# Cross attention steps: maxima of the third tile in front of what a step makes, row scaling and context split in other steps

## The reference, cut to what matters

```python
x = _layernorm(x + attn(x, wq, wk, wv, wo))         # 16 heads of 32, rotary, causal
x = _layernorm(x + xattn(x, ctx, Wq, Wkv, Wout))    # causal: only the first 512 rows of ctx count
x = _layernorm(x + ffn(x, w1, w2, w3))              # w1..w3 = nf4_roundtrip(weight1..3)

# xattn
qp = q @ Wq.T
k, v = split(latent_kv @ Wkv_expand.T, 2)
scores = where(causal, einsum('bhqd,bhkd->bhqk', qh, kh) / sqrt(32), -inf)
out = einsum('bhqk,bhkd->bhqd', softmax(scores), vh) @ Wout.T
```

## Time and profile before

| | us |
|---|---|
| median of 3 runs | 1152.41 (1149.77 to 1152.74) |
| the profiled execution | 1148.54 |
| its span, first to last instruction | 1146.8 |
| batches 4 to 7 (cross attention) | 493.8 to 883 of the span |
| TensorE busy | 1034.3 |
| VectorE busy | 753.6 |
| ScalarE busy | 470.7 |
| GpSimd busy | 457.8 |
| mean granted TensorE clock | 0.975 of full speed |

### The profile page before, as it was taken

One profiled execution on the slowest core, in us unless ns is written; L12 is line 12 of the kernel. 1 busy time (PEld: TensorE's weight loads), 2 busy tenths in 40 slices (PEclk: granted clock), 3 DMA queues, 4 the chain that ended last, 5 costly groups with the idle time before them and its releaser, 6 DMA issues.

```text
span 1146.8 us, 17458 instructions
## 1 busy us (share of the span) xinstructions
PE 1034.3 (90%) x6248; PEld 664.9 (58%) x6248; DVE 753.6 (66%) x1566; ACT 470.7 (41%) x578; POOL 457.8 (40%) x492
## 2 busy tenths in 40 slices
PE   6789898988998898998989889888989999999995
PEld 5545445543555354455556555555646888888884
DVE  6785757656765769548866786887684646364545
ACT  3334353645364556455654555555443211112110
POOL 4446975986289545323242333232367300000000
PEclk9799999999999999999999999999999999999998
DMA  5731466477444854646575565647536301101020
GB/s 207 217 93 31 120 167 171 146 190 211 135 147 121 228 167 125 160 82 162 146 177 126 135 176 141 154 107 196 124 83 204 115 1 57 55 11 64 1 74 37
DMA packets 84290, 145.14 MB, mean 127 GB/s; under 512 B 15416, under 2 KB 32160, under 8 KB 83948
## 3 DMA queue, kind: packets, MB, share of 16 engines
q1 hardware_dynamic: 73180, 111.90, 36.6%
q0 software_dynamic: 9712, 31.34, 9.5%
q10 hardware_dynamic: 1312, 0.79, 0.2%
HBM read 78.09 MB, written 23.73 MB: 89 GB/s over the span
## 4 chain that ended last, share of the span: by engine, by line
PE 47%; DVE 13%; POOL 3%; issue 2%; ACT 2%; DMA 2%; SPq 1%; ACTq 0%; DVEq 0%; POOLq 0%
PE att_pv L1014 7%; PE att_scores L1238 7%; PE att_pv L1238 7%; PE att_scores_T L1268 7%; PE att_scores_T L941 4%; PE att_scores L957 4%; PE att_scores_T L943 3%; PE att_scores_T L942 3%; DVE att_scores L1581 2%; PE att_scores_T L1118 2%; PE att_scores_T L990 2%; DVE att_nf_zone L1737 2%; DVE att_mx L1586 1%; DVE att_x_lo L1526 1%; DMA att_probs<-nf_x 1%
## 5 line engine op out<-in xcount | busy, mean ns | idle before, releaser
L1403 ACT ACTIVATE att_probs<-att_scores_T 128x1024 f32<-128x1024 f32 (+2 forms) x256 | 218.2, 884 | 187.0 <-PE att_scores_T L990 184.2
L1014 PE MATMUL att_pv<-att_probs,att_v 128*32 128x512 f32 (+3 forms) x1024 | 220.0, 546 | 3.8 <-POOL att_probs L796 3.2
L1014 PE MATMUL att_pv<-att_probs,att_ones 128*32 128x512 f32 (+3 forms) x1024 | 219.9, 546 | 0.0
L1586 DVE TENSOR_REDUCE att_mx<-att_scores 128x2 f32<-128x1024 f32 x124 | 151.5, 1222 | 101.1 <-PE att_scores L957 100.4
L957 PE MATMUL att_scores<-att_k_stack,att_q_stack 96*128 96x256 f32 (+1 forms) x504 | 165.5, 401 | 48.3 <-DVE att_mx L1586 21.9
L990 PE MATMUL att_scores_T<-att_q_stack,att_k_stack 97*128 97x512 f32 (+2 forms) x512 | 138.9, 381 | 9.7 <-ACT att_raw L1340 2.3
L1581 DVE CUSTOM_DVE_ANT_0 att_scores<-att_scores,att_cmask 128x128 f32<-128x128 f32 (+3 forms) x256 | 120.4, 508 | 37.0 <-PE att_scores L957 37.0
L957 PEld LDWEIGHTS att_scores<-att_k_stack,att_q_stack 96*128 96x128 f32 x504 | 86.8, 191 | 98.1 <-DVE att_mx L1581 35.3
L796 POOL TENSOR_SCALAR_AFFINE_SELECT att_probs<-att_probs 128x256 f32<-128x256 f32 x128 | 59.2, 463 | 189.2 <-ACT att_probs L1403 186.0
L990 PEld LDWEIGHTS att_scores_T<-att_q_stack,att_k_stack 97*128 97x128 f32 x512 | 85.3, 190 | 52.5 <-issue 17.5
L1487 ACT ACTIVATE att_probs<-att_scores 128x512 f32<-128x512 f32 x44 | 26.3, 598 | 207.7 <-PE att_scores L1238 207.7
(11 more groups left out here) (254 smaller groups left out, 2099.1 us busy)
## 6 DMA issues: line engine op xcount, KB each, us to landing
att_q_stack<-att_q_hi SPq DMA_DIRECT2D x128, 128.0 KB, 3.2
att_probs<-nf_x SPq DMA_DIRECT2D x28, 352.0 KB, 3.6
att_nf_home<-nf_reciprocals POOLq DMA_DIRECT2D x48, 176.0 KB, 4.8
att_q_stack<-att_q_lo SPq DMA_DIRECT2D x64, 128.0 KB, 3.5
att_k_stack<-att_k_hi SPq DMA_DIRECT2D x64, 128.0 KB, 3.4
att_nf_home<-nf_x SPq DMA_DIRECT2D x20, 352.0 KB, 3.7
w_nf<-att_nf_zone SPq DMA_DIRECT2D x192, 22.0 KB, 2.8
att_k_stack<-att_k_hi SPq DMA_DIRECT2D x64, 64.0 KB, 3.3
```

The lines of the kernel that those rows point to most:

```text
L1014: last = T.matmul(pv[HD * j:HD * j + HD, sums, q0:S], lhs, pr[:, at:at + S - q0], start=(t == 0), stop=(t == TT - 1))
L1403: A.activation(probs_of(b, r)[:, 1024 * h:1024 * h + w], bank[:, 0:w], ACT.Exp, scale=SCALE).then_inc(st_free, 1)
L1586: V.tensor_reduce(mx[:, p % 2, :].rearrange("p (r t) -> p r t", r=2)[:, :, t], sco[:, :, :], AX.X, ALU.max).then_inc(sc_free, 1)
```

## The change

Six moves, and no operation is added or taken out:

1. TensorE, step 1 of batches 1 to 7: the third tile's maxima (t = 2) stand ahead of `project_out(b - 1, 0)` and not behind it; VectorE takes them ahead of the round's passes and of the residual.
2. TensorE, cross steps that make something (2 to 6): t = 2 stands ahead of the first half of what is made, and t = 3 between the halves; before it was t = 2 between them and t = 3 behind them. VectorE takes t = 0, 1, 2 in a row, ahead of spread, sums and passes, and t = 3 ahead of the last pass.
3. `scale_rows` of batches 5 and 6 goes from step 5 to step 6, behind `over_sums`, and with it the store on SyncE from step 5 to step 6 (`stored_at`); residual loads go to step 7 (two) and to step 0 (two).
4. `split_context(b + 1)` of batches 4 to 6 goes from the end of step 3 to the end of step 0; GpSimd's `load_context` goes from step 4 to step 1 of the next batch.
5. `begin_spread` in step 3 of cross batches stands behind the maxima of t = 1, and in made steps of t = 2.
6. ScalarE, all cross steps with one round at their end: its pass `exceed(end, 0)` stands behind the fourth exponential, not ahead of it.

```diff
--- before.py
+++ after.py
@@ -148,7 +148,7 @@
 
 def stored_at(b):
 
-    return 5 if late(b) and b != B else 4 if b == B else 3
+    return 6 if B < b < NB - 1 else 5 if late(b) and b != B else 4 if b == B else 3
 
 
 def values_of(b):
@@ -593,9 +593,9 @@
                         scaler_rows(1)
                     if b > 0 and p == stored_at(b):
                         store(b - 1)
-                    for t in {6: (0,), 7: (1, 2)}.get(p, ()) if b != B else ():
+                    for t in (({7: (0, 1)} if B < b < NB - 1 else {6: (0,), 7: (1, 2)}).get(p, ())) if b != B else ():
                         load_residual(b, t)
-                    for t in (3,) if b != B + 1 else range(TT):
+                    for t in range(TT) if b == B + 1 else (2, 3) if b > B + 1 else (3,):
                         if p == 0 and b > 0:
                             load_residual(b - 1, t)
                     if (b, p) == after(*ROUND_STEPS[-1], 1):
@@ -867,7 +867,7 @@
                         pool.wait_ge(st_full, AT["raw", b + 1, f"x{p - 1}"] + 1)
                         if nxt[0] <= NB:
                             load_x(*nxt)
-                    if crossed(b + 1) and b + 2 < NB and p == 4:
+                    if b + 1 == B and p == 4 or crossed(b) and b + 2 < NB and p == 1:
                         pool.wait_ge(c_split, b + 1 - B + 1)
                         load_context(b + 2)
                     if (b, p) == (B - 1, 5):
@@ -1179,20 +1179,27 @@
                     if ahead:
                         weigh(b, p, 0)
                     if p == 1 and b > 0:
+                        maxima(*fore, 2)
                         project_out(b - 1, 0)
-                        maxima(*fore, 2)
                         if mid is not None:
                             rounding(mid)
                         project_out(b - 1, 1)
                         for half in range(2):
                             make(b + 1, whats, half)
+                        maxima(*fore, 3)
+                    elif crossed(b) and whats:
+
+                        maxima(*fore, 2)
+                        make(b + 1, whats, 0)
+                        maxima(*fore, 3)
+                        make(b + 1, whats, 1)
                     else:
                         make(b + 1, whats, 0)
                         if fore and not (crossed(b) and p == 0):
                             maxima(*fore, 2)
                         make(b + 1, whats, 1)
-                    if fore and (whats or p == 1):
-                        maxima(*fore, 3)
+                        if fore and (whats or p == 1):
+                            maxima(*fore, 3)
                     if not ahead:
                         weigh(b, p, 0)
                     weigh(b, p, 1)
@@ -1448,9 +1455,11 @@
                     if mid is not None:
                         for k in scalar_passes(mid):
                             exceed(mid, k)
-                    elif 0 in mine:
+                    elif 0 in mine and not crossed(b):
                         exceed(end, 0)
                     exponential(b, p, 3)
+                    if mid is None and 0 in mine and crossed(b):
+                        exceed(end, 0)
                     if (b, p) == (B - 1, 1):
                         act.wait_ge(wq_in, 32)
                         for h, src in enumerate((rsw, rsum)):
@@ -1801,22 +1810,28 @@
                         turn_first(p - 1)
                     if b > 0 and not late(b) and p == 2:
                         end_spread(range(TT))
-                    if late(b) and p == 3:
+                    if b == B - 1 and p == 3:
                         begin_spread(range(TT))
-                    if (b, p) == (B - 1, 4) or b > B and p == 5:
+                    if (b, p) == (B - 1, 4) or (b, p) == (NB - 1, 5):
                         scale_rows(range(0, 2), TT - 1)
                     if fore:
                         maxima(*fore, 1)
                         largest_behind(b, p, 1)
                     if b > 0 and not late(b) and p == 2:
                         scale_rows(range(TT), TT - 1)
+
+                    quick = crossed(b) and bool(made(b + 1, p))
+                    if quick:
+                        maxima(*fore, 2)
+                    if crossed(b) and p == 3:
+                        begin_spread(range(TT))
                     if late(b) and p == 3:
                         end_spread(range(TT))
                     if b == B and p == 3:
                         scale_rows(range(TT), TT - 1)
                     if b == B - 1 and p == 4:
                         scale_rows(range(2, TT), TT - 1)
-                    if b > B and p == 5:
+                    if (b, p) == (NB - 1, 5):
                         scale_rows(range(2, TT), TT - 1)
                     if p % 2 == 0 and pairs(b, p) > 0:
                         sums_of(G)
@@ -1832,19 +1847,23 @@
                     beside = 0 < b < B - 1 and p == 6
                     if not beside:
                         exceeds(end, (1, 2))
-                    if fore:
+                    if fore and not quick:
                         maxima(*fore, 2)
                         largest_behind(b, p, 2)
+                    if quick:
+                        maxima(*fore, 3)
                     exceeds(end, (1, 2, 3) if beside else (3,))
                     if p % 2 == 0 and pairs(b, p) > 0:
                         over_sums(G)
+                    if B < b < NB - 1 and p == 6:
+                        scale_rows(range(TT), TT - 1)
                     if (b, p) == (0, 2):
                         reciprocals()
                     if crossed(b + 1):
                         for what in made(b + 1, p)[:-1]:
                             cut_raw(b + 1, what)
                     early = bool(made(b + 1, p)) or p == 1
-                    if fore and early:
+                    if fore and early and not quick:
                         maxima(*fore, 3)
                         largest_behind(b, p, 3)
                     if end is not None:
@@ -1857,7 +1876,11 @@
                             cut_raw(b + 1, what)
                         elif what[0] != "v" and b > 0:
                             swap(("raw", b + 1, what))
-                    if crossed(b + 1) and b + 1 < NB and p == 3:
+                    if (b, p) == (B - 1, 3):
+                        split_context(B)
+                    if crossed(b) and b + 1 < NB and p == 0:
+
+                        wait_freed(dve, ("raw", b, "v1"))
                         split_context(b + 1)
             sums_of(KT * NB - 1)
             over_sums(KT * NB - 1)
```

## The result

The changed kernel takes 1167.01 us as a median of four runs (1164.90 to 1169.22), the kernel before 1151.09 us beside it (1147.90 to 1152.74). The ratio is 1.0142 with a 95% interval of 1.0109 to 1.0175, slower by 15.9 us. The forecast was 1168 in a range of 1155 to 1174.

A forecast was written before the change was run, and what follows sets the result against it. TensorE, busy 90% of the span, was taken to bound the kernel, with VectorE setting the pace in steps 2, 4 and 5. Terms summed to +16.3 us on a median of 1152.4, about 1168 us, range 1155 to 1174.

The forecast's parts named there:

- Steps 6 and 7: Batches 5 and 6: rows scaled in step 6 delay the store and SyncE's list behind it; +9.2 and +8.5 us.
- The last term: Batches 5 and 6: from the first pass of step 7 to its end, 4.4 us, ending at 30.0.
- case without the blocking: Rival: rows and GpSimd do not block each other; +8 to +11 us, 1161 to 1163 us; chance 0.22.
- The split: Context split at the end of step 0 meets `weighed`, delaying t = 1 in step 1 of batches 4 to 6; +4.55 us.
- Steps 4: Context split leaves step 4, which gets 1.0 us shorter in each of three batches; -3.0 us.
- ScalarE's pass: Pass behind the fourth exponential: +0.7 us in step 0 of batches 5, 6, 7, +0.3 in step 7 of batch 4; +2.4.
- The clock: Rival: TensorE idles 5 us or more in step 7 and the clock drops behind both long waits; +3, 1171 us; chance 0.10.
- Steps 2, 3, 5 and steps 1 of batches 2 and 3: New maxima order, and rows gone from steps 5: +0.3 steps 2, -0.5 steps 3, -4.7 steps 5, +0.9 those steps 1.
- Step (4, 6): Step 6 of batch 4, forecast 0.4 us shorter.
- step (7, 2): Step 2 of batch 7, where no round follows: the wait before t = 3 goes, -0.9 us.
- a sign of being wrong: The prediction is wrong if steps 2 to 5 give back more than 4 us in a batch.
- The likely case at 0.50: The forecast itself, 1168 us with its own range 1163 to 1173; chance 0.50.

The follow-up runs named there:

- the second: The changed kernel once more with no edit, for a second profile: 1162.77 us.
- the second of before: The kernel before once more with no edit, for a second profile: 1148.05 us.
- rows_only: The kernel before with the third move alone (rows of batches 5 and 6 and their store in step 6): 1165.71 us, ratio 1.0128.
- store_behind: The changed kernel with SyncE's store of batches 5 and 6 behind step 7's round, their residual loads all in the next step 0: 1153.0 us, ratio 1.0017.
- store_gpsimd: The changed kernel with the store of batches 5 and 6 issued by GpSimd behind `weighed` in step 6, not by SyncE: 1151.83 us, ratio 1.0021.
- rows_ahead: The changed kernel with the four scaled rows of step 6 ahead of `over_sums`: 1161.9 us, ratio 1.0093.
- best_guess: store_behind with the sixth and fourth moves undone and the four rows of step 6 ahead of `over_sums`: 1148.21 us, ratio 0.9991.
- best_three: best_guess with step 1 of batches 1 to 3 in old order, step (4, 5)'s 1 MB load earlier, third move undone: 1151.98 us, ratio 1.0018.

## Why the prediction was right, and where only its sum was

**Steps 6 and 7, +17.7 forecast.** They grew by 8.2 and 7.5 us in the first profile, 8.0 and 9.0 in the second against the second of before: 15.7 and 17.0. Step by step, from the start of step 6 at 780.50: round's rows issued 3.4 us in (forecast 4.2), first pass 7.2 (8.0), first scaled row 10.6 (11.4), rows 4.1 us (4.3), last row 14.7 (15.8), first pass of step 7 23.9 (25.6), end 28.9 (30.0). Counted from its own start, step 7 had its rows issued at 7.3 us (forecast 8) and its first pass at 10.7 (forecast 12 to 13). The mechanism is shown at each link: rows_only puts the loss in this move, store_behind and store_gpsimd put it in the list order, and rows_ahead shows the mutual blocking. The terms are a little high since SyncE is 0.8 us earlier than I took it and the way behind the store is 9.2 us, not 9.65. The last term is too low: from the first pass of step 7 to its end it took 5.0 us and not 4.4, and TensorE ran at half clock from 803.23 on. That the rows also stand in front of `scale_rounded`, and cost 1.2 to 1.6 us by that, I had left out. Under the longer wait it was hidden. Without that wait it is most of what remains, and with the rows ahead of `over_sums` (best_guess) it is gone.

The Trainium skill, page "SBUF — State Buffer", section "Who interferes with whom", describes an exclusive lock on the ports that VectorE and GpSimd share. By that rule the trace agrees (4.08 against 1.91 us for the same four instructions, and 1.48 against 1.29 for GpSimd's).

One by one, the four rows took 0.50, 1.50, 0.83 and 1.49 us in the changed kernel. The last three ended at 793.01, 793.76 and 795.17, each 0.28 us after one of GpSimd's three had ended (792.73, 793.48, 794.89). So each of them waited out one whole instruction, and this case's own rows show it. Lifting this took 5.1 us off the median (rows_ahead). The prediction calls its case without the blocking "11 us lower"; its own terms (5 and 3 us) make that 8.

**The split, +4.55 forecast.** The place was right, the size was not. In batches 5 and 6 its second instruction began 0.4 us behind the start of GpSimd's last and waited for the rest of it alone: 1.65 us in place of 0.77. In batch 4 the first one waited, 1.28 us in place of 0.42. The split cost 0.7 us in each step 1, 2.1 us in all. In batch 6 TensorE's t = 1 came 1.1 us later and not 1.6, and of this only 0.7 reached the length of the step, where the sum took the whole delay for length. How much of the 0.7 the blocking makes has not been isolated: the forecast without it was 0.6. Steps 4 gave back 2.3 us and not 3.0.

**ScalarE's pass, +2.4 forecast.** It cost 2.6 us, measured by undoing it.

**The clock, a rival at 0.10.** It came. TensorE stood idle for 6.3 to 6.4 us before `rounding` in both long steps 7, and ran at its lower level (1.2 GHz) for about 10 us from the middle of that time on, into the next step 0. A window of the changed kernel over that stretch in batch 6 shows a mean of 0.53:

```profile
803.00:814.00 11.00, 6.88 (x46) 4.57 (x47) 5.55 (x19) 3.85 (x5) 0.81 (x2) 0.53 0.82 217
```

Step (6, 0) took 1.1 and (7, 0) 1.2 us more than their 11.45 at full clock. That is 2.3 us on top of the forecast in the first profile, and 1.0 in the second.

**Steps 2, 3, 5 and steps 1 of batches 2 and 3.** Forecast +0.3 (three batches), -0.5, -4.7 and +0.9. Measured +0.1 in each step 2 at full clock, -0.45, -4.8, and +0.4 twice against the second profile of before. These held. Step (4, 6), forecast at -0.4, was 1.0 us longer in the first profile and the same in the second, and step (7, 2) was 0.6 shorter (forecast 0.9). What I had not foreseen: the kernel before had a stretch at half clock in three of four steps 2 of batches 5 and 6, and of the kernels with the new order only best_three had one there, at no cost (10.95 us, as at full clock). That is -2.7 us in steps 2 of the first pair of profiles. It also met a sign of being wrong that the prediction had named, more than 4 us given back by steps 2 to 5 in a batch: they gave back 4.6 and 4.3 us in the first pair, and 4.4 and 2.3 in the second. Without the half clock in steps 2 of the kernel before it is about 3 us.

Step (7, 3) is missing from the sum. At full clock it took 8.04 us in the second profile of the kernel before, and 10.00 and 8.87 in the two of the changed kernel. Seven of the eight other kernels with the new order have 10.00 to 10.02, and best_three 10.26. In the list of this step only the fifth move changed. TensorE waits there 1.88 us for GpSimd's mask and, before t = 3, for VectorE, whose maxima of t = 2 now stand behind all the small operations of the spread:

```profile
859.40 1.01 PE L957 MATMUL att_scores<-att_k_stack,att_q_stack 96*128 96x512 f32 x2 [1.61 <-DVE att_mx L1590]
```

What of it the fifth move costs by itself has not been tested. Steps 3 to 6 of batch 7 together took 2.0 us more in the first pair, the half clock in them included.

So each term but that of step (4, 6) has its sign, the largest was 1 to 2 us too high, the split 2.5 too high, the clock 2.3 too low, step (7, 3) was left out, and these meet. The steps of batches 4 to 7 together took 14.5 us more in the first pair of profiles and 17.8 in the second, where the sum has 15.4. Of the 16.4 us between the first two spans, 5.0 lie in batch 0, which no edit touches, and batches 1 and 2 give 2.8 back. That the total lies within 1 us of the forecast is luck: the sum was good to 3 us or so. The likely case at 0.50 was the right one, with the clock added.

## What to carry to other kernels

A queue that issues in order is an engine like the others: when a store in it waits for a result, read what stands behind it, and put the store behind whatever the next step needs, or on another queue. Moving work to where its engine has slack is not free if it then runs beside work of another engine that holds it up. The same rows cost 1.9 us ahead of the instruction that woke GpSimd, and 4.1 behind it. A gain of some tenths in a step is found by comparing the steps of two profiles, since the runs of this kernel spread over 10 us.

## What the runs showed of the hardware

A VectorE instruction on a 128x3 tile can take 2.4 us. In batch 0, in a part that no edit touches, the two profiles of the kernel before differ in which engine came first. In the first, VectorE's instruction began 0.01 us ahead of GpSimd's and took 0.17 us (and the next one 2.25):

```profile
111.88 0.17 DVE L1691 TENSOR_SCALAR att_nf_zone<-att_nf_zone 128x3 bf16<-128x3 f32 x1
112.08 2.25 DVE L1693 CAST att_nf_zone<-att_nf_zone 128x3 f32<-128x3 bf16 x1
```

```profile
111.89 2.42 POOL L739 TENSOR_TENSOR att_turned<-att_raw,att_rope_tab 128x1024 f32<-128x1024 f32 x1
```

In the second, GpSimd's began 0.03 us ahead, and the 128x3 instruction and a later one both waited:

```profile
111.14 2.40 DVE L1691 TENSOR_SCALAR att_nf_zone<-att_nf_zone 128x3 bf16<-128x3 f32 x1
113.57 0.17 DVE L1693 CAST att_nf_zone<-att_nf_zone 128x3 f32<-128x3 bf16 x1
113.77 2.67 DVE L1696 TENSOR_TENSOR att_nf_zone<-att_nf_zone 88x384 bf16<-88x384 bf16 x1
```

```profile
111.11 2.40 POOL L739 TENSOR_TENSOR att_turned<-att_raw,att_rope_tab 128x1024 f32<-128x1024 f32 x1
```

Step (0, 4) was 3.6 us longer in the second, and a stretch at half clock followed in steps 4 to 7 of this batch in 12 of the 13 profiles, the first one alone excepted. The wait shows as the instruction's own duration and not as idle time. That this alone makes up the 10 us over which the runs spread has not been tested.
